# A decoder layer in one program: the last context chunks, the routing and the last expert in another order

## The reference

```
x = _layernorm(x + _L0_attn_ref(x, ...))             # causal attention, 16 heads of 128
x = _layernorm(x + _L0_xattn_ref(x, ctx, ...))       # linear attention over 375 context rows per batch
x = _layernorm(x + _L0_ffn_ref(x, ...))              # 8 experts, each row goes to its best 2

# inside _L0_xattn_ref
k, v = jnp.split(kv @ Wkv.T, 2, axis=-1)             # phi(k) = where(k > 0, k + 1, exp(k)), phi(q) likewise
attn = einsum(phi(q), einsum(phi(k), v)) / (einsum(phi(q), sum(phi(k))) + EPS)
out = attn * sigmoid(query @ Wg.T + bg) @ Wo.T

# inside _L0_ffn_ref
top_vals, top_idx = jax.lax.top_k(h @ router_weight.T + router_bias, 2)
scores = softmax(top_vals) put at top_idx
glu = min(gate, 7) * sigmoid(1.702 * min(gate, 7));  act = (clip(up, -7, 7) + 1) * glu
out = sum over experts of scores * (act @ down_proj + down_proj_bias)
```

## Time and profile before

| | |
|---|---|
| median of 3 runs | 924.97 us (924.18 to 927.13) |
| profiled execution: its own time | 927.66 us |
| its span, first to last instruction | 925.8 us |
| TensorE busy | 851.2 us, 92% |
| VectorE / ScalarE / GpSimd busy | 468.0 / 307.6 / 101.4 us |
| mean granted TensorE clock | 0.957 of full |

### The profile page before, as it was taken

How to read it: one execution, slowest core, us unless ns; L and a number is a source line. 1 busy time by engine, 2 the same in 40 slices (tenths; PEclk the granted TensorE clock), 3 DMA queues, 4 the chain that set the end, 5 groups by cost and what they waited for, 6 DMA issues and landing times.

```text
span 925.8 us, 12579 instructions
## 1 busy us (share of the span) xinstructions
PE 851.2 (92%) x4967; PEld 746.3 (81%) x4967; DVE 468.0 (51%) x853; ACT 307.6 (33%) x666; POOL 101.4 (11%) x95
## 2 busy tenths in 40 slices
PE   6999999999999999899999999899778799999990
PEld 6999999989898989888898777777546788888870
DVE  3435454453636462757622344444553666666634
ACT  4343333242423332422442221121113345554530
POOL 0000000000000000000000010011030133333343
PEclk9999999999999999999999999999856899999995
DMA  9940715341201002013100111100546366655226
GB/s 324 358 148 1 248 62 198 112 148 36 92 1 61 32 10 105 1 46 126 34 1 1 34 34 58 57 23 24 205 151 172 117 188 188 188 162 163 70 28 186
DMA packets 34462, 96.99 MB, mean 105 GB/s; under 512 B 5721, under 2 KB 7769, under 8 KB 31713
## 3 DMA queue, kind: packets, MB, share of 16 engines
q1 hardware_dynamic: 30592, 87.70, 27.5%
q0 software_dynamic: 3808, 8.46, 4.2%
HBM read 64.03 MB, written 32.12 MB: 104 GB/s over the span
## 4 chain that ended last, share of the span: by engine, by line
PE 76%; DVE 9%; ACT 6%; issue 6%; DMA 2%; POOL 1%; POOLq 0%; SPq 0%; DVEq 0%
PE bank L275 61%; PE bank L592 3%; PE bank L539 2%; PE bank L624 2%; ACT w_gu L944 2%; DVE w_gu L1239 1%; PE bank L582 1%; PE bank L726 1%; PE bank L515 1%; DVE prob L1277 1%; DVE hh L1703 1%; ACT x_g L1153 1%; PE bank L696 1%; DMA y_acc<-y,meta 1%; DVE up L1694 1%
## 5 line engine op out<-in xcount | busy, mean ns | idle before, releaser
L275 PE MATMUL bank<-w_kv,cT 128*125 128x512 f32 x576 | 145.0, 402 | 0.9 <-DVE acc L1266 0.9
L275 PE MATMUL bank<-xT,w_qkv 128*128 128x448 f32 x672 | 137.6, 365 | 0.1
L275 PEld LDWEIGHTS bank<-xT,w_qkv 128*128 128x128 f32 x672 | 126.1, 188 | 10.6 <-ACT qT L965 0.5
L275 PEld LDWEIGHTS bank<-w_kv,cT 128*125 128x125 f32 x576 | 104.8, 187 | 24.9 <-issue 1.3
L275 PE MATMUL bank<-x_g,w_gu 128*128 128x288 f32 x768 | 111.3, 304 | 11.7 <-DVE w_gu L1239 6.9
L275 PEld LDWEIGHTS bank<-x_g,w_gu 128*128 128x128 f32 x768 | 106.5, 194 | 14.9 <-DVE w_gu L1239 9.9
L275 PE MATMUL bank<-w_qkv,xT 128*112 128x256 f32 x672 | 85.4, 283 | 0.0
L275 PE MATMUL bank<-w_o,zT 128*128 128x512 f32 x336 | 79.7, 395 | 0.5 <-DVE acc L1554 0.5
L275 PEld LDWEIGHTS bank<-w_qkv,xT 128*112 128x112 f32 x672 | 79.9, 175 | 0.0
L418 POOL TENSOR_TENSOR ln_rs<-ln_ve,half 128x1 f32<-128x1 f32 (+2 forms) x16 | 12.7, 794 | 589.1 <-DVE ln_ve L1359 589.1
L275 PEld LDWEIGHTS bank<-w_o,zT 128*128 128x128 f32 x336 | 62.1, 189 | 14.6 <-DVE acc L1266 1.5
(11 more groups left out here) (144 smaller groups left out, 1174.2 us busy)
## 6 DMA issues: line engine op xcount, KB each, us to landing
x_rows<-blank SPq DMA_DIRECT2D x9, 2084.0 KB, 18.1
raw_gu<-in_w_gu_dram SPq DMA_DIRECT2D x8, 2048.0 KB, 7.7
raw_w<-in_w_qkv_dram SPq DMA_DIRECT2D x21, 512.0 KB, 6.9
raw_dn<-in_w_down_dram SPq DMA_DIRECT2D x8, 1024.0 KB, 5.8
raw_c<-in_ctx_t_dram SPq DMA_DIRECT2D x8, 750.0 KB, 4.3
raw_o<-in_w_o_dram SPq DMA_DIRECT2D x8, 512.0 KB, 3.5
xg<-x_rows SPq DMA_DIRECT2D x8, 512.0 KB, 6.7
raw_kv<-in_w_kv_dram SPq DMA_DIRECT2D x2, 1024.0 KB, 6.6
```

Of the source, the lines that this page charges most:

```text
L275: last = nc.tensor.matmul(mm_out, lhs(a, k), rhs(b, k), start=(k == 0 and i == 0), stop=(k == n - 1 and i == 2))
```

## The change

In words:

- **Chunks and batches.** Chunks 21 and 22 stood together in the iteration of batch 4, and chunk 23 in straight code with batches 5 and 6. Now chunks 21, 22 and 23 stand one to each of the iterations of batches 4, 5 and 6, so `attended`, `turn_atn`, `turn_x2` and `router` of a tile come with fewer chunks around them, and `cross_out(5)` and `cross_out(6)` stand before most of the routing of tiles 5 and 6. The order on ACT, DVE and POOL is rewritten to match.
- **Routing banks.** From `turn_score(0)` on, the routing takes banks 6, 4, 5, 7 in turn in place of 6 and 7. Banks 4 and 5 are free once the last `sums_out` has read them (a new wait in `take`), and TensorE's wait before the experts covers banks 0 to 5 in place of 0 to 3.
- **Bias products.** `turn_score`/`down_bias` of tiles 1 to 6 stand behind the routing of tile 6; before, tiles 1 to 3 were among it. SP's `base_store` of all seven tiles stands behind the loads of the first three experts' tables.
- **Expert weights.** For e of 2 and more the quarters of expert e + 1 are split from q = 1 on (before: q = 2), on ACT and DVE; the last quarter no longer stands between two `y_evac`.
- **Last expert.** `down(6)` stands between the second and the third gate/up quarter of expert 7 in place of behind the fourth; the `y_evac` of expert 6 and the split of expert 7's down weights move up to the same place on ACT and DVE. POOL's queue of the expert part is as it was.

The diff, cut to what these words rest on (the matching rewrites of the bank lists and of the engines' straight code after the loop are left out where "..." stands):

```
-    CHUNKS = ((6, 7, 8, 9), (10, 11, 12, 13), (14, 15, 16, 17), (18, 19, 20), (21, 22))
+    CHUNKS = ((6, 7, 8, 9), (10, 11, 12, 13), (14, 15, 16, 17), (18, 19, 20))
...
+            last = [("st", 0), ("rk", 4), ("db", 0), ("t1", 5), ("rt", 5), ("t1", 6), ("rt", 6),
+                     ("rk", 5), ("st", 1), ("rk", 6), ("cnt", 0), ("db", 1)]
+            for n in range(2, NT):
+                last += [("st", n), ("db", n)]
+            for i, (what, n) in enumerate(last):
+                yield what, n, (6, 4, 5, 7)[i % 4]
...
+        def split_from(e):
+            return 2 if e == 1 else 1
...  (SP)
-            base_store(0)
-            base_store(1)
...
-            for n in range(2, NT):
+            for n in range(NT):
                 base_store(n)
...  (PE)
                 if turn > 1:
                     pe.wait_ge(free[k], turn - 1)
+                elif k in (4, 5):
+                    pe.wait_ge(m["sum_out"], 2 * NB)
...
+            for b in range(4, 7):
+                n = b + 17
+                attended(b)
+                sums(n - 1)
+                ctx_k(n)
+                turn_atn(b)
+                if b > 4:
+                    turn_x2(b - 2)
+                ctx_v(n)
+                if b > 4:
+                    router(b - 2)
+                if b < 6:
+                    cross_out(b - 1)
+                if b == 5:
+                    rank(3)
             sums(23)
             turn_score(0)
...
-            for k in range(4):
+            for k in range(6):
                 pe.wait_ge(free[k], LAST[k])
...
-                if e:
-                    for k in range(3):
-                        down(e - 1, k)
+                    if e and q == (3 if e + 1 < NE else 1):
+                        for k in range(3):
+                            down(e - 1, k)
...  (ACT: x2_copy, gu_high and score_copy after the context)
             score_copy(0)
             a_high(7)
+            gu_high(0, 0, 0)
             x2_copy(5)
-            gu_high(0, 0, 0)
+            x2_copy(6)
...  (ACT, experts)
+                    if q == 2 and not more:
+                        for k in range(3):
+                            y_evac(e - 1, k)
+                        dn_high(e, e % 2)
...
-                        if e:
-                            gu_high(e + 1, (e + 1) % 2, q - 2)
+                    if more and e and q >= split_from(e):
+                        gu_high(e + 1, (e + 1) % 2, q - split_from(e))
...  (DVE, experts)
+                    if q == 2 and not more:
+                        dn_low(e, e % 2)
...
-                        if e:
-                            gu_low(e + 1, (e + 1) % 2, q - 2)
+                    if more and e and q >= split_from(e):
+                        gu_low(e + 1, (e + 1) % 2, q - split_from(e))
```

More of the change, by code:

```diff
@@ L433, in _ @@
             inverse_std(0, 4, NT, 2)
-            for n in range(4):
+            for n in range(3):
                 inverse_std(1, n, n + 1, n + 3)
                 scatter(n)
+            inverse_std(1, 3, 4, 6)
             inverse_std(1, 4, 5, 7)
+            scatter(3)
             inverse_std(1, 5, 6, 8)
+            inverse_std(1, 6, 7, 9)
             scatter(4)
-            inverse_std(1, 6, 7, 9)
             scatter(5)
@@ L1113, in _ @@
                         c_high(n // CT + 1)
-            top_tanh(3)
+            for b in range(4, 7):
+                feature_k(b + 17)
+                a_high(b)
+                if b > 4:
+                    x2_copy(b - 2)
+                    top_tanh(b - 2)
             def use(c):
@@ L1623, in _ @@
                         c_low(n // CT + 1)
-            choose(3)
-            attended(5)
-            assign(3)
-            phi(23)
-            gated(5)
-            a_low(5)
-            v_copy(23)
-            attended(6)
-            cross_add(4)
-            gated(6)
-            a_low(6)
+            for b in range(4, 7):
+                attended(b)
+                if b == 4:
+                    sums_out(6)
+                else:
+                    x2_norm(b - 2)
+                phi(b + 17)
+                gated(b)
+                a_low(b)
+                v_copy(b + 17)
+                if b == 5:
+                    choose(3)
+                if b < 6:
+                    cross_add(b - 1)
+                if b == 5:
+                    assign(3)
             sums_out(7)
-            x2_norm(4)
-            cross_add(5)
+            choose(4)
             attended(7)
-            bias_add(0)
-            x2_norm(5)
-            bias_add(1)
-            choose(4)
             gated(7)
             a_low(7)
+            cross_add(5)
+            assign(4)
+            x2_norm(5)
+            cross_add(6)
+            bias_add(0)
+            x2_norm(6)
             choose(5)
-            assign(4)
+            choose(6)
+            assign(5)
+            assign(6)
             gu_low(0, 0, 0)
-            cross_add(6)
-            assign(5)
-            x2_norm(6)
             gu_low(0, 0, 1)
-            bias_add(2)
-            choose(6)
-            bias_add(3)
-            assign(6)
-            gu_low(0, 0, 2)
-            gu_low(0, 0, 3)
             dve.wait_ge(*ready("cnt", 0))
@@ L1667, in _ @@
             nc.vector.tensor_copy(more_i[:, :], most[:, 4:5]).then_inc(m["more_ok"], 1)
[L1668 removed]
+            for n in range(1, NT):
                 bias_add(n)
+                if n in (2, 3):
+                    gu_low(0, 0, n)
             gu_low(1, 1, 0)
```

87 lines of the change are left out of this document (27 added, 60 removed).

## The result

The changed kernel takes 917.6 us (median of 4 runs, 915.42 to 918.16) against 924.76 us (4 runs, 924.18 to 927.13) on the same chip: ratio 0.9899, 95% interval 0.9878 to 0.9919. It is 1.0% faster. The median is 5.7 us above the forecast of 911.9, and 0.1 above the stated range of 906.5 to 917.5; counted by the ratio, from the median before, it is 924.97 x 0.9899 = 915.6, which lies in the range and 3.7 above the forecast.

The account below looks back on a forecast made before the run. Bound by TensorE, waiting and slow-clocked in routing and standing still 5% among the experts. Terms -12.3 - 6.0 + 5.2 = -13.1 us, from the median 924.97 to 911.9 us; range 906.5 to 917.5.

Parts of the forecast that it names:

- Routing, -12.3: Routing up to expert 0: earlier `cross_out(6)` and four banks start the gathers near 688 us, 12.3 us sooner.
- Rival B: Routing: clock falls already at `cross_out(5)`, so routing gains only 7.5 us; 916.7 us in all, chance 0.14.
- The clock rule: Routing's bias products: by the skill's rule activity releases the half clock (-15.6 us); by the profile's rows it stays (-12.3).
- Expert weights, -6.0: Expert loop: splitting one quarter earlier removes TensorE's waits for split weights, five of 1.15 us and one of 0.4.
- Rival C: Expert loop: early quarter holds up each clamp, VectorE stays last, loop gains 1 us; 916.9 us, chance 0.08.
- Last expert, +5.2: Expert 7: TensorE stands still 4.2 us for the uncovered hidden chain, then runs `down(7)` at half clock; costs 5.2 us.
- The second mechanism offered: Program's end: POOL's additions of expert 7 wait for those of expert 6 to land, ending 4.6 us later.
- Rival E: First experts: half clock runs on through gate/up and down, one whole turn giving +17.8 us; 929.7 us, chance 0.03.

Follow-up runs that it names:

- the late down split: Changed kernel with the old last expert, VectorE's down split behind quarter 0's clamp and ScalarE's third scaling ahead of the down cast: ratio 0.9790, 907.31 us.
- the filler: Unread matmuls in TensorE's waits from `cross_out(6)` to expert 0's gate/up, on the late down split with expert 7's down split at quarter 1: 0.9788 against 0.9802.
- the square: New routing throughout, against the kernel before: quarter and last expert old 0.9864; only quarter new 0.9843; only last expert new 0.9918; both new 0.9899.

## Why the prediction came out as it did

Counted by the ratio (915.6 us) the range held the time, though the narrower band given to the forecast itself, 909.5 to 914.5, did not. Routing and last expert were right in mechanism and size. The forecast's sum was -13.1; the profiled executions differ by 9.4 in span, and 3.3 of the missing 3.7 us are one term: routing gave 12.4 (the 12.8 at expert 2 less the 0.4 that belong to the weights), the weights 2.7, and the last expert cost 5.7.

- **Routing, -12.3: right.** -12.9 us at gate/up of expert 0, -12.8 at expert 2, 12.6 by the experiments. The small steps held: `cross_out(6)` at 659.50 at full clock, the slots of tile 6 within a microsecond of the forecast, pairs of 2.72 us. That the trace comes within 0.6 us of the term is luck in part: the gathers' 0.7 us of delay and 1.2 us gained behind them nearly cancel, and in other traces of the same routing `cross_out(6)` starts anywhere from 657.68 to 661.58 us. The 12.6 of the runs is the firmer figure. Rival B (the clock falls at `cross_out(5)` behind a wait) fell: the wait was 0.80 us, and the product took 3.04. Not foreseen: gate/up of expert 1 takes 9.28 us for 8.13, where gate/up of expert 0 had gained 0.6 (8.02 for 8.66). This share differs from one execution to the next: in the trace with the late down split, in which TensorE's order is the same up to there, the two take 8.38 and 7.96 us.
- **The clock rule.** The half clock held through the bias products, as the rows said, and the filler shows that it would have held with TensorE 97% busy. The working by rule, -15.6 for routing, did not come true.
- **Expert weights, -6.0: the failed step; measured -2.3 in the trace (expert 2 to 7: 117.52 us for 119.83) and -0.4 in the turn before, 1.8 to 1.9 by the square.** The step said: "So a wait of 1.15 us goes five times", with "Late next is VectorE, by 0.1 us". The first part is true. But the working followed the moved quarter and the clamps on VectorE alone, and let the down split, which comes forward with them, be free. It moved ahead of POOL's second addition, held it for 1.8 us, and so brought `pr` so late that `hidden(0)` ran into POOL's second product and was held too. That came back over the clamp of quarter 2 and the split of the first gathered piece to TensorE: 0.67 us ahead of the third piece, and 0.2 at the turn's end, where the last split now ends as the down product does. First turn 22.90 (forecast 22.8; the addition held, `hidden(0)` not), the other four 23.66: 4 x 0.86 = 3.4 us. With the split out of the way it is 22.70, five waits gone as the step had it. Nor was the lower bound (-3.6, clamps slipping 0.5 us) wide enough.
- **Rival C** had the size nearly right for a wrong reason: not the quarter, but the down split against another engine's queue. The row that would have shown it was in the trace before: the third addition's 2.19 us beside a split, where the second took 1.55.
- **Last expert, +5.2: right.** +5.7 in the trace, 5.0 to 5.2 by the square; 4.30 us of bare wait and 1.6 of half clock. 0.6 us of the wait is the late clamp of quarter 3 (879.63, the quarter's product having ended at 879.02), as the prediction had it. The second mechanism offered, POOL's own chain, was not the limit.
- **Rival E** did not come: the clock was back at full in expert 0 and again behind the first product of expert 1.
- **Small slips of the working.** The steps to the rank of tile 6 add up to 672.1, not 672.3 (671.7 in the trace); a pair at full clock is 1.77 us, not 1.7; rival B's term is -7.4, not -7.5. None changes a rival or the range.

## What to carry to other kernels

When a step on one engine is moved earlier, all that stands behind it on that engine moves too; lay its new times beside what other engines do there, GpSimd above all, and look for two instructions whose order of start is turned round. Before a rearrangement is judged on its sum, time its parts alone: here 12.6 us of gain, 5 us of loss and a part worth a third of its promise were one result of 1%. And do not pull a product forward if what it covered is the last chain of the program.

## What the runs showed of the hardware

- **An indirect DMA on POOL that starts inside a VectorE product of two SBUF operands waits until that is over.** Addition 3.39 us for 1.56 beside a split of 2.29 that had started 0.32 us earlier: it ends 1.42 us behind the split's end, nearly its own length. Started 0.62 or 0.72 us ahead of the split, it is not held. The product `pr` on POOL is held alike (2.53 for 0.90). The other way round the two kinds differ: `hidden(0)` on VectorE, started inside a `pr`, is held (1.05 for 0.45), but a split started 0.62 or 0.72 us into an addition takes its usual 2.29 us. The Trainium skill, "SBUF — State Buffer", section "Who interferes with whom", says that a VectorE instruction with two SBUF inputs contends with a GpSimd instruction that reads SBUF, that the shared ports are an exclusive lock, and that the order of issue decides who blocks. For `pr` the traces agree both ways; for the addition they agree where the split comes first, and where the addition comes first they show no hold. The same section infers that generating a DMA's descriptors is not stalled by such a product. These additions, which read their row numbers from SBUF, are stalled as a whole; the traces do not part the reading from the generating.
- **The half clock, once there, can outlast products without gaps.** In the filled kernel 0.50 from 672.5 to 690 us, with TensorE busy throughout with bias products of 8 rows, score transposes and filler of 128.
